# Four blocks in one program: semaphores counted on, the next block's rows turned behind the last down product, the last norm inside the next block

## What is computed

```python
# x (32,64,128), ctx (32,64,128), masks, gates g_xattn, g_ffn (4 each)
x = x + tanh(g_xattn[0]) * decayed_sum(ctx**2) * norm(x)      # opens a block
x = x + tanh(g_ffn[0])   * moe16(norm(x))                     # "ffn0": 16 experts, 2 chosen, plus a shared one
x = x + tanh(g_xattn[1]) * attention(norm(x), ctx)            # 16 heads of 8
x = x + tanh(g_ffn[1])   * moe8(norm(x))
x = x + tanh(g_xattn[2]) * attention(norm(x), ctx, mask)
x = x + tanh(g_ffn[2])   * lora_moe4(norm(norm(x)))
x = x + tanh(g_xattn[3]) * perceiver(norm(x), norm(ctx), mask) # 16 heads of 64
z = z + attention(z); z = rms(z, n1); z = z + moe8(z)          # "ffn3", z kept in xn
x = x + tanh(g_ffn[3])   * rms(z, n2)                          # the last norm; x is the output
```

## Time and profile before

| | before |
|---|---|
| median of 3 runs | 1726.91 us (1722.79 to 1728.47) |
| the profiled execution | 1730.62 us |
| its span on the core | 1728.8 us |
| PE busy | 1432.1 us (83%) |
| DVE busy | 1084.8 us (63%) |
| ACT busy | 733.3 us (42%) |
| POOL busy | 409.7 us (24%) |
| mean granted clock of PE | 0.933 of full speed |

### The profile page before, as it was taken

How to read it: one execution, slowest core, us unless ns; L and a number is a source line. 1 busy time by engine, 2 the same in 40 slices (tenths; PEclk the granted TensorE clock), 3 DMA queues, 4 the chain that set the end, 5 groups by cost and what they waited for, 6 DMA issues and landing times. The chain is left out here.

```text
span 1728.8 us, 28859 instructions
## 1 busy us (share of the span) xinstructions
PE 1432.1 (83%) x11038; PEld 938.7 (54%) x11038; DVE 1084.8 (63%) x3318; ACT 733.3 (42%) x1397; POOL 409.7 (24%) x318
## 2 busy tenths in 40 slices
PE   5788988886887988797878898889797799888877
PEld 3455644564654654466555564446555466445645
DVE  3456765767636666576754676577654667657666
ACT  0244434562234533564324543456432454256532
POOL 1122311630031330351014031054012223017200
PEclk9899989999989999999889999999897999999989
DMA  9000000000000000000000000000000000000000
GB/s 329 0 1 1 1 1 0 2 2 16 1 7 1 1 1 1 1 2 16 2 7 1 1 1 1 1 1 2 16 1 7 1 1 1 1 1 2 1 16 7
DMA packets 16824, 19.60 MB, mean 11 GB/s; under 512 B 3352, under 2 KB 15400, under 8 KB 16172
## 3 DMA queue, kind: packets, MB, share of 16 engines
q1 hardware_dynamic: 16688, 17.75, 3.1%
HBM read 16.70 MB, written 1.05 MB: 10 GB/s over the span
## 5 line engine op out<-in xcount | busy, mean ns | idle before, releaser
L251 POOL TENSOR_TENSOR root<-variance,minus_half 128x2 f32<-128x2 f32 (+1 forms) x75 | 58.1, 775 | 743.8 <-DVE variance L268 472.6
L1068 ACT ACTIVATE work<-bank,w_f 128x512 f32<-128x512 f32 x128 | 87.9, 687 | 118.8 <-PE bank L1005 118.5
L1016 PEld LDWEIGHTS bank<-w_f1d,work 128*128 128x128 f32 x1024 | 119.4, 192 | 15.3 <-issue 15.3
L1563 ACT ACTIVATE work<-work,small 128x128 f32<-128x128 f32 x256 | 78.3, 388 | 113.4 <-DVE small L1696 113.4
L1016 PE MATMUL bank<-w_f1d,work 128*128 128x129 f32 x1024 | 119.5, 275 | 0.0
L1005 PE MATMUL bank<-xnT,w_f 128*128 128x512 f32 x256 | 117.7, 606 | 0.0
L1618 POOL TENSOR_TENSOR small<-small 128x16 f32<-128x16 f32 x32 | 92.9, 2902 | 102.8 <-DVE small L1654 101.6
L1399 PE MATMUL bank<-w_x,cxT 128*128 128x512 f32 x128 | 71.7, 688 | 31.9 <-DVE work L1667 27.1
L1097 POOL TENSOR_TENSOR small<-small,minus_half 128x4 f32<-128x4 f32 x32 | 57.6, 1799 | 140.1 <-DVE small L1136 140.1
L1653 DVE TENSOR_REDUCE small<-work 128x16 f32<-128x1024 f32 x48 | 58.4, 1216 | 51.6 <-ACT work L1532 40.3
L620 DVE TENSOR_REDUCE small<-bank 128x8 f32<-128x512 f32 x96 | 65.5, 682 | 33.7 <-PE bank L487 33.7
(11 more groups left out here) (289 smaller groups left out, 3323.5 us busy)
## 6 DMA issues: line engine op xcount, KB each, us to landing
w_f<-in_f_dram SPq DMA_DIRECT2D x1, 2616.0 KB
w_f<-in_f_dram SPq DMA_DIRECT2D x1, 2180.0 KB, 26.6
w_x<-in_x_dram SPq DMA_DIRECT2D x1, 2115.0 KB
w_l<-in_l_dram SPq DMA_DIRECT2D x1, 2088.5 KB, 21.3
w_f1d<-in_f1d_dram SPq DMA_DIRECT2D x4, 512.0 KB
work<-in_x_dram SPq DMA_DIRECT2D x5, 256.0 KB, 3.0
work<-in_ctx_dram SPq DMA_DIRECT2D x5, 256.0 KB, 3.6
out_dram<-x SPq DMA_DIRECT2D x4, 256.0 KB, 2.3
```

What stands on the lines that cost most here:

```text
L1016: pe.matmul(z_of(e, t)[:, 0:129], hT[e % 2][:, c, t * P:(t + 1) * P], w_f1d[:, c, e, :], start=(c == 0), stop=(c == 3))
L1068: act.activation(hT[e % 2][:, c, :], banks[n % 3][:, :], ACT.Relu, bias=k_f1["b1"][:, n:n + 1]).then_inc(hT_ready, 1)
L1563: ins = act.activation(s_sb[b % 2][:, c * P:(c + 1) * P], s_sb[b % 2][:, c * P:(c + 1) * P], ACT.Exp, bias=negmax[b % 2][:, c:c + 1])
```

## The change

It does four things.

1. **Semaphores count on.** Each semaphore is made once, with a number of increments per block (`"q_done:2"`); waits inside the loop use `due(sem, n)`, which is n plus the block's number times that count, and waits of work for the next block use `ahead`. `clear`, its DVE instructions and its barriers are gone; all four blocks stand in one `nc.Block()`. One barrier stays between `prepare` and the first block, and one at the end.
2. **Rows turned without a border.** PE's turning of `xn_next` waits for a new semaphore `opened`, given by DVE once `xn_next` is normed; it stands right behind the last down product. The router behind it waits, among others, for the last addition of DVE to `xn` (`prev`, the semaphore `added`).
3. **The last norm goes into the next ffn0.** In the first three blocks `rms_last` is no longer run at the end of ffn3 but in four pieces behind gate_up(0) to gate_up(3) of the next block; its root is given by POOL behind weighted(1). The old `x` is stored after the last piece; DVE waits for that store at step 6. The copy `x<-x_next` (L909) is gone; the first addition of ffn0 reads `x_next` and writes `x`. POOL's small memset (L889) stands behind its wait for the router's factors.
4. **The last block prepares nothing** (`more` is false): the context work and `open_rows` are left out there, and no padding rows are loaded.

```diff
-                pe.wait_ge(rows_ready, 2 * turn + pair + 1)
+                if turn == 0:
+                    pe.wait_ge(opened, due(opened, 1))
+                else:
+                    pe.wait_ge(rows_ready, due(rows_ready, 2 * turn + pair - 1))
...
             yield from layer_norm(dve, link, [(x_next, xn_next, t) for t in range(TILES)], by_pool=True)
+            dve.sem_inc(opened, 1)
...
 def ffn0
-                    turn_pairs(pe, prev, turn_no, xn_next)
+                    turn_pairs(pe, None, turn_no, xn_next)
+                    pe.wait_ge(c_taken, due(c_taken, 2))
+                    pe.wait_ge(kv1.v_ready, due(kv1.v_ready, TILES))
+                    if prev is not None:
+                        pe.wait_ge(prev, 8 * i)
                     pe.wait_ge(l0_loaded, 16)
...
-                    pool.memset(h_shared[:, :, 352:384], 0.0).then_inc(rest_cleared, 1)
-                    pool.wait_ge(comb_ready, 1)
+                    pool.wait_ge(comb_ready, due(comb_ready, 1))
+                    pool.memset(h_shared[:, :, 352:384], 0.0)
...
+                        if (t, g) == (0, 1) and i > 0:
+                            give_root(pool, 4)
...
-                    dve.sem_inc(rows_ready, 2)
-                    dve.wait_ge(stored, 16 * i + 16)
-                    link(dve.tensor_copy(x[:, :, :], x_next[:, :, :]))
...
+                    last_rows = iter(()) if i == 0 else rms_last(dve, link)
                     for s in range(n + 2):
                         if s < n:
                             gate_up(s)
+                            some(last_rows, 1)
                             some(next_rows, 3)
+                        if s == 6 and i > 0:
+                            dve.wait_ge(stored, 16 * i)
...
-                            dve.scalar_tensor_tensor(x[:, t, :], banks[6 + t % 2][:, 0:D], tg[:, 4:5], x[:, t, :],
+                            dve.scalar_tensor_tensor(x[:, t, :], banks[6 + t % 2][:, 0:D], tg[:, 4:5], x_next[:, t, :],
...
 def ffn3
+            more = i + 1 < BLOCKS
-                        if s == 2:
+                        if s == 2 and more:
                             turn_context(pe)
...
-                    run(rms_last(dve, link))
+                    if not more:
+                        run(rms_last(dve, link))
...
-        def clear(sems):
-                nc.vector.sem_clear(range(a, b))
-            nc.all_engine_barrier()
```

More of the change, by code:

```diff
@@ L954, in body @@
                 ends.append(Ends((hid_ready, len(steps) - 1), (taken, 4)))
-            stage("cleared routed halves sig comb up sil weighted hid turned hidT down taken", body)
+            stage("routed:1 halves:1 sig:1 comb:1 up:20 sil:20 weighted:16 hid:20 turned:20 hidT:20 down:20 "
+                  "taken:4", body)
             return ends[0]
```

597 lines of the change are left out of this document (300 added, 297 removed).

## The result

The changed kernel took 1698.28 us (median of 4 runs, 1696.73 to 1703.48), the kernel before 1725.53 (4 runs, one more than ahead of the prediction, 1722.79 to 1728.47). The ratio is 0.9847, with a 95% interval from 0.9819 to 0.9875: 27 us less, or 1.5%. The forecast was 1696.9, within 1691 to 1703.

The account below looks back on a forecast made before the run. Taken as the bound: borders where all engines run out of work, 10.19 us three times. Three borders at 8.2 net (24.6) plus start 0.6 plus last block 4.8 make 30.0 us off 1726.91: 1696.9 us, range 1691 to 1703.

Parts of the forecast that it names:

- The border, 8.9 us each, three times: Between blocks: score copy at 472.9 in place of 481.82, 8.9 us less; 8.0 if the router ran at half clock.
- The root, 0.1 us late: Norm's root on POOL in ffn0: just covered by a half-clock up product, 0.1 us late; up to 0.9 at full clock.
- The sum held by key_blocks, 0.6 us: Norm's sum on DVE in ffn0: held up beside POOL's key_blocks, making turn(4) late, 0.6 us; bounds 0 and 1.4.
- ffn0 as a whole: Norm inside ffn0: root 0.1 and sum 0.6 us per border, scaling and store 0.
- rival B: Norm paid in ffn0's first steps: root uncovered (0.9), sum costs 1.4; time 1701.7 us; chance 0.20.
- The start, 0.6: Between prepare and PE's start: clears and one barrier go, 0.6 us less, between 0.2 and 0.9.
- The last ffn3, 4.8: Last block's ffn3: preparation pieces removed, 4.5 us after overlaps, plus a PE wait for DVE; 4.8, bounds 4.2 and 5.5.
- A: Norm in ffn0 is free: sum not held up or its delay not reaching PE, root covered; 1694.8 us; chance 0.22.
- A stage far from the borders changed its length: Sign of being wrong: a stage far from the borders has another length in the changed profile; no size given.
- At 0.50 for more than some 5 us after turn(0): Sign of being wrong: clock at 0.50 for more than some 5 us after turn(0) in ffn0.
- C: Slower: clock stays at 1.2 GHz through most of ffn0, up to 18 us a border, time 1751; chance 0.03.
- D: Border does less: barrier only hid a late DVE or other engine; 3 us a border leave 21, 1706; chance 0.04.

Follow-up runs that it names:

- the second series: The changed kernel run again, nothing altered: 1700.61 us (6 runs, 1688.36 to 1703.01), ratio 0.983 to the kernel before.
- The shifts: The changed kernel with three, six or nine more small DVE copies behind every ffn0's score copy: 1698.13, 1698.42 and 1703.12 us.
- the kernel with the late wait: The changed kernel with PE's wait for DVE's last addition moved from the router to ffn0's first turning: 1699.4 us, ratio 0.9833.
- the split norm: The changed kernel with that wait late, squares, mean and root behind the last addition, scaling behind gate_up(0), sum behind gate_up(2): 1689.9 us, ratio 0.9785.
- the filling products: The changed kernel with four useless PE products ahead of turn(0) in blocks 1 to 3: 1696.33 us, ratio 0.9815; together with the split norm 1682.57.
- six copies: The changed kernel with six more small DVE copies behind the score copy of every ffn0: 1698.42 us, ratio 0.9847.
- Nine copies: The changed kernel with nine more small DVE copies behind the score copy of every ffn0: 1703.12 us, ratio 0.9868.

## Why the prediction was right, point by point

- **The border, 8.9 us each, three times.** Right. From the last addition's end to the score copy it was to be 0.2 + 1.07, and was 1.45, 1.35 and 1.36; from the down product's end the three borders gave 8.74, 8.88 and 9.17, together 26.8, where three times 8.9 are 26.7. PE's gap there is 1.07 and 0.98 us, about the 1 us that was named. The wait for the last addition took the barrier's place as said; the run with that wait moved prices it at 0.36 us. The router ran at the full clock, as I had chosen against 8.0.
- **The root, 0.1 us late.** By sign right, by size and constancy not: 0.5 late in block 1, where the clock was still full and up(2) took 1.14 us (476.91 to 478.05), covered in blocks 2 and 3, where it took 1.9. The condition that rival B named decides it block by block.
- **The sum held by key_blocks, 0.6 us.** Right in mechanism and size: 1.93 us in place of 0.75, and a wait of PE of 0.46, 0.43 and 0.56. Taking the meeting away gave about 0.6 us a block where the low clock in the stage was the same, by few stages.
- **ffn0 as a whole.** 0.7 us a block were forecast, 2.1 in three; the three stages grew by 0.8 together (38.55, 39.53, 38.64 against 37.88, 39.04, 38.96). The forecast missed that the stages before also had low clock from their border (17 to 20 us at 1.2 GHz), which the new border mostly spares. So a cost of the norm and a gain of the clock lie in this one number. The cost also has no one size: at full clock throughout, the norm where the changed kernel has it costs 2.1 us a block (38.34 against 36.26 with the norm split).
- **The start, 0.6.** PE starts 0.30 us after `prepare`, where it was 1.05, 0.75 less. At the score copy it is 0.78, but over the runs with this start that copy comes anywhere from 63.5 to 66.5.
- **The last ffn3, 4.8.** The step that was mis-sized: 5.45, both in the changed kernel and in the kernel before with that part alone. The six pieces took 4.7 from start to start, and 4.5 was what the records less their overlaps had given. What else was too small is the addition for DVE: 0.3 for waits that went with `open_rows`, where 0.7 went. I had counted the one wait that the profile names, and the last four down products gave 0.6 (7.94 to 7.31); that the rest of it is DVE's is not shown.
- **The sum.** 26.8 + 5.45 + 0.8 for the start - 0.8 for ffn0 + 0.3 between score copy and weighted(0) - 1.2 between ffn0 and ffn3 is, within rounding, the 31.3 us between the two spans; 30.0 were forecast. The medians differ by 27.2. The profiled execution of before was 5.1 us above its own median, that of after 1.0 above; taking the difference from the one and the level from the other assumed that the two profiles sit alike over their medians. The terms of the sum were 1.3 too small, the median of the kernel before came out 1.4 lower with its fourth run, and the place of the two profiles over their medians took 4.1 the other way: together the forecast for the median was 1.4 too low. That it came so near is in part luck: errors of 1 to 4 us offset each other, and runs of the changed kernel lie 7 us apart (15 in the second series), as far as rivals A (1694.8) and B (1701.7). The time alone could not have told the forecast from these two; the traces do.
- **"A stage far from the borders changed its length."** This was named as a sign of being wrong, and it occurred: the perceiver of block 2, 5.2 us. The shifts show that it is no effect of the change as such. The sign was badly chosen, because such a stage takes one of several lengths in any kernel here.
- **"At 0.50 for more than some 5 us after turn(0)."** This sign occurred too, narrowly: 5.5 us in block 2, against about 3.4 in the other two. The low clock through most of ffn0 that rival C named did not follow.
- **The rivals.** A (norm free) is out by the sum's 1.93 us. B's full price is out: the root was late by 0.5 us in one block of three, and turn(4) waited 0.43 to 0.56, not 1.4. C is out: the low clock in ffn0 was 3.4 to 6.8 us. D is out: the score copy comes 1.35 to 1.45 us after the last addition, so the barrier hid no later wait.

## What to carry to other kernels

At a border that drains every engine, price each thing on the chain from the last result to the next one needed, and then look at the clock: here the norm was 3.0 us of it, the clears 1.5, and the barrier 4.3, of which under 1 was the barrier itself and the rest the turning and the router, which it put behind the norm instead of beside it. From the turning to the score copy these took 3.54 us at half speed (473.53 to 477.07) and 2.35 at full speed in the kernel with the late wait, so 1.2 of it is the clock. When an edit removes one of two limits and the time does not move, look for which other limit the freed engine ran into before calling the first worthless; the split norm and the filling products alone left ffn0 at 38.53 and 38.34 us on average, against 38.58 and 38.91 in the changed kernel's two profiles, and together they brought it to 36.26. And compare kernels that differ by less than 5 us stage by stage in the trace, not by the median: a shift of a microsecond moves where the clock is low, and that can take or give back more than the edit.

## What the runs showed of the hardware that I had not expected

- 5.5 us of added work on the path that everything waits for left the time as it was (1698.42 against 1698.28 and 1700.61), because the stages behind met the clock otherwise: between ffn0 and ffn3 they took 1296.7 us in the profile with six copies, 1305.2 and 1310.6 in those without. The same 944 products of the perceiver took 110.8 to 116.7 us of PE, and the stage 133.5 to 139.8. Nine copies, 8.2 us, did cost some of it (1703.12).
- The hold-up between DVE and POOL is about what is left of the instruction that came first, not so much for each instruction behind it. The sum of 0.75 us, started 0.52 into key_blocks, became 1.93; of four scalings, 1.13 together, one alone was held and they became 3.05, with POOL's instruction itself at 1.95 in place of 1.90. Where POOL's came second it was the one that grew, to 2.35.
- The pause of almost 4 us in front of turn(0) lowered the clock only at its end or behind it (in block 1 1.00 in 472 to 476, then 0.78 and 0.65; in block 2 0.50 from 1.3 us before turn(0) on). Products of 3.6 us put into the pause kept PE from standing still there, and the clock was then full through ffn0, and up(2) started no later (5.9 us after the score copy, with the products and without).
